# Batch 0 of the last loop: half of the quad sums moved to GpSimd, the residual moved behind the next unit's pair sums

## What is computed

```python
h = gelu(batchnorm(conv1x1(h, w_c2, b_c2), bn2_g, bn2_b))       # 4 x 128 channels: ll, lh, hl, hh
y00 = (ll + lh + hl + hh) * 0.5
y01 = (ll + lh - hl - hh) * 0.5
y10 = (ll - lh + hl - hh) * 0.5
y11 = (ll - lh - hl + hh) * 0.5
x = x + interleave(y00, y01, y10, y11)                          # back to 256 x 256
x = x + blur4x4(group_norm(x))
```

## Time and profile before

| | us |
|---|---|
| median of three runs | 5783.29 (5782.67 to 5785.78) |
| the profiled execution's own time | 5775.72 |
| its span | 5773.8 |
| VectorE busy in the span | 4367.2 |
| TensorE busy in the span | 5208.6 |
| ScalarE, GpSimd busy in the span | 3695.3, 2060.5 |

### The profile page before, as it was taken

One profiled execution on the slowest core, in us unless ns is written; L12 is line 12 of the kernel. 1 busy time (PEld: TensorE's weight loads), 2 busy tenths in 40 slices (PEclk: granted clock), 3 DMA queues, 4 the chain that ended last, 5 costly groups with the idle time before them and its releaser, 6 DMA issues. The chain is left out here.

```text
span 5773.8 us, 71505 instructions
## 1 busy us (share of the span) xinstructions
PE 5208.6 (90%) x18152; PEld 3158.9 (55%) x18152; DVE 4367.2 (76%) x5317; ACT 3695.3 (64%) x5001; POOL 2060.5 (36%) x1388
## 2 busy tenths in 40 slices
PE   2888888977889988897679999999999999999999
PEld 1333333323555555554246666666666666666677
DVE  8555555347889888884998888888888888888833
ACT  1333333356667666663678878788887877878754
POOL 0000000047677666660013333333333333333354
PEclk9999999998999999998889999999999999999999
DMA  9999999732333333323999999999999999999986
GB/s 367 382 379 381 374 380 383 295 134 78 97 94 104 102 95 95 95 84 133 327 346 402 403 397 402 389 401 397 388 389 393 398 397 391 396 391 395 398 299 227
DMA packets 829437, 1729.46 MB, mean 300 GB/s; under 512 B 50048, under 2 KB 587008, under 8 KB 718464
## 3 DMA queue, kind: packets, MB, share of 16 engines
q1 hardware_dynamic: 755328, 1389.81, 66.0%
q10 hardware_dynamic: 73728, 335.58, 14.1%
HBM read 1050.95 MB, written 674.23 MB: 299 GB/s over the span
## 5 line engine op out<-in xcount | busy, mean ns | idle before, releaser
L1041 POOL TENSOR_TENSOR y_lo<-y_centred_tile,y_hi 128x1024 fp32r<-128x1024 f32 x512 | 1039.9, 2052 | 1721.5 <-ACT y_centred_tile L1377 1405.7
L1256 PE MATMUL blur_psum<-y_hi,band_hi 128*128 128x512 f32 x4096 | 1128.8, 417 | 8.8 <-DVE y_tile L1134 7.4
L1239 PE MATMUL conv_psum<-u_in,w_conv 128*128 128x512 f32 x2048 | 966.6, 615 | 107.3 <-DVE pair_sums L1112 84.8
L1256 PE MATMUL blur_psum<-y_lo,band_hi 128*128 128x512 f32 x4096 | 1042.7, 397 | 7.2 <-POOL y_lo L1041 6.8
L1256 PEld LDWEIGHTS blur_psum<-y_hi,band_hi 128*128 128x128 f32 x4096 | 765.7, 188 | 279.0 <-issue 100.8
L1112 DVE TENSOR_TENSOR pair_sums<-gelu_out,conv_psum 128x512 f32<-128x512 f32 x1024 | 653.5, 684 | 302.7 <-ACT conv_psum L1347 292.9
L1256 PEld LDWEIGHTS blur_psum<-y_lo,band_hi 128*128 128x128 f32 x4096 | 769.7, 188 | 200.6 <-POOL y_lo L1041 16.2
L1134 DVE SCALAR_TENSOR_TENSOR y_tile<-blur_psum,rstd_all,y_tile 128x1024 f32<-128x1024 f32 x512 | 639.6, 1277 | 159.3 <-PE blur_psum L1256 152.0
L1347 ACT ACTIVATE gelu_out<-conv_psum,bn_shift,bn_scale 128x512 f32<-128x512 f32 x512 | 397.2, 776 | 525.8 <-PE conv_psum L1239 503.4
L1239 PEld LDWEIGHTS conv_psum<-u_in,w_conv 128*128 128x128 f32 x2048 | 397.6, 197 | 553.6 <-issue 395.9
L558 POOL TENSOR_TENSOR tap_products<-tap_products 128x512 f32<-128x512 f32 x512 | 652.2, 1274 | 128.9 <-ACT tap_products L786 108.8
(11 more groups left out here) (165 smaller groups left out, 5434.1 us busy)
## 6 DMA issues: line engine op xcount, KB each, us to landing
x_tile<-x SPq DMA_DIRECT2D x256, 1024.0 KB, 10.1
y_scratch<-x_tile ACTq DMA_DIRECT2D x256, 1024.0 KB, 8.5
y_tile<-y_scratch SPq DMA_DIRECT2D x512, 512.0 KB, 10.9
out<-y_tile SPq DMA_DIRECT2D x512, 512.0 KB, 10.0
x_stream<-x SPq DMA_DIRECT2D x192, 1024.0 KB, 11.4
x_resident<-x SPq DMA_DIRECT2D x160, 1024.0 KB, 11.1
z_scratch<-z_tile ACTq DMA_DIRECT2D x256, 256.0 KB, 7.1
z_in<-z_scratch SPq DMA_DIRECT2D x256, 256.0 KB, 3.5
```

Source lines behind the costliest of these rows:

```text
L1041: nc.gpsimd.tensor_tensor(y_lo[:, h, part, 2:2 + W], y_c[:, part, :], y_hi[:, h, part, 2:2 + W].bitcast(F32), ALU.subtract).then_inc(s_lo, 1)
L1239: nc.tensor.matmul(cv[s][:], w[:, s * C:(s + 1) * C], u_t[:, k % US, :], start=True, stop=True).then_inc(s_mm, 1)
L1256: ins = nc.tensor.matmul(bl[t][:, 2 * c:2 * c + 2, :], wt[:, kw, :], y[:, h, ch:ch + 2, kw:kw + W], start=(m == 0 and kw == 0), stop=(m == ...
```

## The change

For batch 0 alone there are now two sets of pair sums and two of quad sums; the second sets lie in slots 4 and 5 of `y_tile`. In pass k of VectorE's loop it makes the pair sums of unit k, then waits for `s_q1` and does the residual of unit k - 1, then makes the even quad sums of unit k in one instruction. GpSimd makes the odd quad sums of unit k in one instruction once VectorE's even ones are done. A 33rd pass does the last residual. The other batches are as before; ScalarE, TensorE and SyncE are unchanged.

```diff
--- before.py
+++ after.py
@@ -886,6 +886,8 @@
         spread_s = sb("gn2_seam_spread", [128, 2, NQ])
         rest_n = sb("rests_of_partition", [128, 1])
         rest_i = sb("rests", [1, 1], mybir.dt.int32)
+        sums_of = [sums_t[:], y_t[:, 4].rearrange("p t c w -> p (t c w)").rearrange("p (s n) -> p s n", s=4)]
+        quads_of = [d_t[:], y_t[:, 5].rearrange("p t c w -> p (t c w)")]
         cv = [ps(f"conv2_psum{s}", [128, BANK]) for s in range(4)]
         bl = [ps(f"blur_psum{t}", [128, GRP, W]) for t in range(2)]
         small = cv[2]
@@ -904,6 +906,7 @@
         s_ge = sem("gelu2_done")
         s_s1 = sem("pair_sums_done")
         s_s2 = sem("quad_sums_done")
+        s_q1 = sem("odd_sums_done")
         s_y = sem("y_ready")
         s_sq = sem("y_squared")
         s_yst = [sem(f"y_stored{i}") for i in range(XS)]
@@ -937,6 +940,12 @@
         ov = out.rearrange("b c h w -> (b c) h w")
         block = ctx.enter_context(nc.Block())
 
+        def quad_views(k):
+
+            dv = quads_of[k % 2].rearrange("c (i a j e) -> c a e i j", a=2, e=2, j=W2)
+            sv = sums_of[k % 2].rearrange("c (a p) (i j) -> c a p i j", p=2, j=W2)
+            return dv[:, :, 0], dv[:, :, 1], sv[:, :, 0], sv[:, :, 1]
+
         def phases(engine, body):
             body(0, FIRST)
             body(1, SECOND)
@@ -1048,6 +1057,11 @@
 
             def body(b, phase):
                 for k in range(LAG_SPLIT if phase == END else UNITS):
+                    if phase == FIRST:
+
+                        pool.wait_ge(s_s2, k + 1)
+                        _, odd, first, second = quad_views(k)
+                        nc.gpsimd.tensor_tensor(odd, first, second, ALU.subtract).then_inc(s_q1, 1)
                     if group_at(b, phase, k, LAG_SPLIT) is not None:
                         rests(b, phase, k)
                     if k == 1 and SECOND <= phase <= DRAIN:
@@ -1104,12 +1118,12 @@
             dve.wait_ge(s_p, 5)
             nc.vector.tensor_copy(rest_i[:], cv[0][0:1, 0:1]).then_inc(s_ready, 1)
 
-            def pairs(b, k):
+            def pairs(b, k, sums):
                 for p in range(2):
 
                     dve.wait_ge(s_ge, b * (4 * UNITS) + 4 * k + 2 * p + 2 + 4)
                     for m, op in enumerate((ALU.add, ALU.subtract)):
-                        ins = nc.vector.tensor_tensor(sums_t[:, 2 * m + p, :], g_t[:, k % 2, p, :], cv[2 * p + 1][:], op)
+                        ins = nc.vector.tensor_tensor(sums[:, 2 * m + p, :], g_t[:, k % 2, p, :], cv[2 * p + 1][:], op)
                     ins.then_inc(s_s1, 1)
 
             def quads(b, k):
@@ -1120,11 +1134,17 @@
                     ins = nc.vector.tensor_tensor(dv[:, :, e], sv[:, :, 0], sv[:, :, 1], op)
                 ins.then_inc(s_s2, 1)
 
-            def residual(b, k):
+            def even_quads(k):
+
+                dve.wait_ge(s_s1, 2 * k + 2 + 4)
+                even, _, first, second = quad_views(k)
+                nc.vector.tensor_tensor(even, first, second, ALU.add).then_inc(s_s2, 1)
+
+            def residual(b, k, quads):
                 i = k % XS
                 dve.wait_ge(s_x[i], b * (16 * UNITS // XS) + 16 * (k // XS) + 16)
                 dve.wait_ge(s_s2, b * UNITS + k + 1)
-                nc.vector.scalar_tensor_tensor(x_t[:, i, :], d_t[:], 0.5, x_t[:, i, :],
+                nc.vector.scalar_tensor_tensor(x_t[:, i, :], quads, 0.5, x_t[:, i, :],
                                                ALU.mult, ALU.add).then_inc(s_y, 1)
 
             def take(b, k, t):
@@ -1146,9 +1166,19 @@
                 c = b - 1
                 done = SECOND <= phase <= DRAIN
                 gl = Chain(dve, s_gl, c * LINKS_GN)
+                if phase == FIRST:
+                    for k in range(UNITS + 1):
+                        if k < UNITS:
+                            pairs(0, k, sums_of[k % 2])
+                        if k >= 1:
+                            dve.wait_ge(s_q1, k)
+                            residual(0, k - 1, quads_of[(k - 1) % 2])
+                        if k < UNITS:
+                            even_quads(k)
+                    return
                 for k in range(LAG_BLUR if phase == END else UNITS):
                     if phase <= MIDDLE:
-                        pairs(b, k)
+                        pairs(b, k, sums_t)
                     if done and k == 1:
 
                         dve.wait_ge(s_sq, b * UNITS + XS)
@@ -1172,7 +1202,7 @@
                         ins.then_inc(s_gsp, 1)
                     if phase <= MIDDLE:
                         quads(b, k)
-                        residual(b, k)
+                        residual(b, k, d_t[:])
                     if done and k == 1:
                         dve.wait_ge(s_gp, b * 2 - 1)
                         gl.link(nc.vector.tensor_copy(st[:, 5:6], small[:, 0:1]))
```

## The result

The changed kernel takes 5834.73 us, the median of six runs (5832.2 to 5851.68); the kernel before, run beside it, 5782.98 us. The ratio is 1.0094, 95% interval 1.0081 to 1.0107: **51.75 us slower**, against 48 forecast. Its profiled execution took 5833.91 us with a span of 5832.0.

A forecast was written before the change was run, and what follows sets the result against it. VectorE was taken to bound batch 0 before the change, a ring through ScalarE after it. Start 1.1 us later, 30 periods of 8.80 and a last 5.6 make 48 us slower: 5783.3 + 48 = 5831 us, range 5822 to 5843.

The forecast's parts named there:

- The bound: Batch 0 of the last loop before the change: VectorE sets the pace, busy 222.58 of 227 us, 7.185 us a unit.
- the ring: Batch 0: GELUs, second pair sums, previous unit's residual, its store and square, next GELUs, without overlap; 8.80 us a unit, chance 0.91.
- The ring's terms: Batch 0, per unit: signal 0.03, pair sums 1.28, overlap -0.08, residual 2.29, store and square 2.42, GELUs 2.83; 8.77 us.
- the lower bound: Batch 0's period with the residual starting 0.08 us before the pair sums' shown end: 8.77 us, against 8.96 if 0.11 behind.
- ScalarE's part: Batch 0, per unit: store issue and square of k - 1, 2.42 us, then GELUs of k + 1, 2.83; together 5.25.
- The start: Start of batch 0's loop: unit 0's residual ends about 2721.4, 1.1 us later; GpSimd's odd sums must be done by 2719.1.
- GpSimd's instruction: Odd quad sums in batch 0: taken as 2.0 us, between 1.27 and 3.0; hidden in the loop up to 5.2 us.
- The end: End of batch 0: 30 periods, 264.0 us, then 5.6 us for the last residual, which ends at 2991.0.
- Covers: Batch 0: added waits, early loads (268 GB/s) and matmuls, even at TensorE's 1.2 GHz clock, all hidden at no cost.
- A: Batch 0: VectorE still sets the pace, or transfers do, 6.0 to 6.5 us a unit; 5747 to 5762 us, chance 0.04.
- B: Batch 0: GpSimd's odd sums take longer than 5.2 us and join the ring; at 6.5 us, 5879 us, chance 0.03.
- C: After batch 0: the 48 us is given back by slack later; 5783 us, chance 0.02.

The follow-up runs named there:

- run 1: Changed kernel with VectorE making both quad sums and GpSimd idle in batch 0, residual still one unit late: 5837.76 us against 5786.19, ratio 1.009.
- run 2: Changed kernel with the residual back in its own unit, GpSimd keeping the odd quad sums: 5830.32 us against 5786.19, ratio 1.008.
- Run 3: Changed kernel with the square of unit k - 2 ahead of the store of k - 1 in batch 0: 5783.01 us against 5786.19, ratio 0.9993.
- run 4: Changed kernel with ScalarE's store and square two units back in batch 0: 5771.58 us, ratio 0.9978; repeated unedited, 5779.56 us, ratio 0.9979.
- Run 5: Changed kernel with GpSimd's odd quad sums of batch 0 made twice in a row: 5841.79 us against 5791.01, ratio 1.0094.
- run 9: Kernel of run 2 with GpSimd starting when the pair sums are ready, beside VectorE's even sums: 5824.37 us against 5788.94, ratio 1.0066.

## Why the prediction was right

**The bound.** VectorE set the pace of batch 0, as I said, and losing 1.22 us of its work gained nothing, since the reordering closed a ring through ScalarE. Runs 1 and 2 separate the two halves of the change: the lag alone gives the changed kernel's period to 0.01 us, and GpSimd alone gives 8.41 us, with VectorE waiting for it in every unit.

**The ring's terms.** Forecast 0.03 + 1.28 - 0.08 + 2.29 + 2.42 + 2.83 = 8.77, taken as 8.80; measured 8.76 in the unit shown and 8.776 on average. The residual starts 0.08 us before the shown end of the pair sums, so the lower bound held. Run 3 takes one term out and the period falls by 1.9 us; run 4 takes ScalarE's part out and the ring is gone.

**The start.** Forecast 1.1 us later, measured 1.20 (14.04 from the mark to the first residual, before 12.84). GpSimd's first odd sums ended at 2725.78, 0.06 us after the pair sums; with 2.0 us instead of 2.37 they would not have mattered.

**GpSimd's instruction.** This is the term that was mis-sized: taken as 2.0 us, it takes 2.35. The row had the operands and the count but not the stride of the output, and 0.35 us is what that and the other differences cost. It counts once in full, in the last period, which took 5.89 us for 5.6. Run 5 shows that the ring doesn't feel it. The estimate of 2.25 us from the Trainium skill (GPSIMD Engine Reference, section Elementwise, side-by-side cycle accounting) was nearer here than the row.

**The end.** Forecast 264.0 + 5.6 from first to last residual; measured 263.27 + 5.89. With the start that is 47.6 us between the marks for 48. That it is so close is in part luck: the period was taken 0.02 us too long, 0.7 us in all, and the start and the last period 0.1 and 0.3 us too short.

**Covers.** The loads came early, and TensorE's lower clock was hidden, as forecast: the granted clock averaged 0.79 in batch 0 for 0.87 before, so more of it at the lower of the two levels (1.2 and 2.4 GHz), and from 2740 to 2980 us no GELU waited for a matmul and nothing for a load.

**The rivals.** A (VectorE sets the pace) is refuted for the changed kernel and is what run 4 turns on by moving ScalarE's finish: most of its units then last 5.9 us for the 6.0 of the rival. Its range for the total was 5747 to 5762, and version 4 reaches 5771.58 and 5779.56, in part because late loads bring the mean period to 6.4 to 6.8 us, where the rival had 6.0 to 6.5. The rule of the Trainium skill (Perfetto Trace Analysis, section Identifying the Most-Contended Engine), to relieve the engine with the highest occupancy first, names the right engine and holds once the ring is open; by itself it gave the wrong sign. B (GpSimd in the ring) didn't occur. C (given back) didn't either.

**What stays open.** About 4 us behind batch 0: 2837.0 us from the 32nd residual to the end, against 2833.0 and 2834.8 in two profiles of the kernel before. The trace shows where they are not. From the 32nd residual to the first one of batch 3 it is 720.56 us before and 720.54 after; the difference comes later. The first residuals of batches 3 and 4, kernel before:

```profile
3661.33 2.29 DVE L1127 SCALAR_TENSOR_TENSOR x_tile<-quad_sums,x_tile 128x2048 f32<-128x2048 f32 x1
...
4024.70 2.29 DVE L1127 SCALAR_TENSOR_TENSOR x_tile<-quad_sums,x_tile 128x2048 f32<-128x2048 f32 x1
```

and changed kernel:

```profile
3715.51 2.29 DVE L1147 SCALAR_TENSOR_TENSOR x_tile<-quad_sums,x_tile 128x2048 f32<-128x2048 f32 x1
...
4083.07 2.29 DVE L1147 SCALAR_TENSOR_TENSOR x_tile<-quad_sums,x_tile 128x2048 f32<-128x2048 f32 x1
```

Batch 3 takes 363.4 us there and 367.6 here, though its code is the same in both. Over all eleven profiles batches 2 to 6 take between 363.4 and 370.3 us, with no pattern by kernel that I can see, so scatter explains a difference of this size. Against it stands that all nine profiles with an edited batch 0 lie above both of the kernel before. Two are few, and I have no mechanism.

## What to carry to other kernels

Before moving a step behind another on one engine, follow who releases that other one: if a second engine does, and its program holds its next work behind the moved step, the move closes a ring whose length is a plain sum, and taking work off an engine that is not in that sum then gains nothing (VectorE's odd quad sums here), while taking a term out of it does (run 3). Offload and reordering should be priced apart. When the ring closes, move the second engine's dependent step back by one more unit too: that one edit turned 1.0094 into 0.9978 here.

## What the runs showed of the hardware that I had not expected

- GpSimd's subtraction of 128x1024 elements took 2.35 us with a float32 output at a stride of two elements, 2.0 us in the rests of later batches, whose output has no gaps and another type (fp32r). No run separates the stride from the type.
- Side by side with a VectorE instruction that also reads two SBUF tensors, GpSimd waited 1.05 us of VectorE's 1.23 and VectorE none (run 9). In a later batch of the kernel before both were stretched: the residual took 3.97 us for 2.29, and two of GpSimd's rests 6.63 for 4.0. There GpSimd's first rest was under way when the residual began, and the residual ended before the second rest did, so each may have waited for the other in turn. The Trainium skill (Perfetto Trace Analysis, section Optimizing Scalar/DVE Operations) says that the two share a read port of SBUF and that moving work between them might not help; run 9 agrees for two instructions side by side, and in the changed kernel the order of waits keeps them apart.
- The square begins 0.39 us after the store's issue in 30 of the 31 units of batch 0, and 0.66 us after it in the 16th. The kernel before has the same 0.66 us in its 16th unit. In the changed kernel that period is 9.04 us long; the other 29 are 8.76 to 8.78.
